# Relational graph convolution on one core: dense block products in float32r, 512 columns wide, on rows split into two parts

## What is computed

```python
h = x @ W                                       # GCN layer
deg_inv_sqrt = where(deg > 0, rsqrt(max(deg, 1)), 0)
out = segment_sum(h[src] * (deg_inv_sqrt[src] * deg_inv_sqrt[dst])[:, None], dst)
x = layernorm(x + out)

def rgcn_layer(X, W, root, bias, gamma, beta):  # 4 of these
    h = einsum('ni,rio->rno', X, W)             # 4 relations
    agg = segment_sum(h[etype, src] * inv_deg[:, None], dst)
    out = agg + X @ root + bias
    out = elu((out - mean) * rsqrt(var + eps) * gamma + beta)
    return out + X
x = layernorm(x + rgcn_layers(x))
```

## Time and profile before

| | us |
|---|---|
| median of 3 runs | 5869.68 (5861.25 to 5871.9) |
| span of the profiled execution | 5905.4 |
| sorting, count building | to about 1400 |
| GCN pass (stretch 1404 to 2282) | 878.0 |
| relational pass 1 (2296 to 3200.7) | 904.7 |
| last pass (5004 to 5884) | 880.0 |

### The profile page before, as it was taken

One profiled execution on the slowest core, in us unless ns is written; L12 is line 12 of the kernel. 1 busy time (PEld: TensorE's weight loads), 2 busy tenths in 40 slices (PEclk: granted clock), 3 DMA queues, 4 the chain that ended last, 5 costly groups with the idle time before them and its releaser, 6 DMA issues.

```text
span 5905.4 us, 80081 instructions
## 1 busy us (share of the span) xinstructions
PE 4806.4 (81%) x20415; PEld 3355.2 (57%) x20415; DVE 3711.0 (63%) x9969; ACT 1418.0 (24%) x3629; POOL 3267.9 (55%) x3256
## 2 busy tenths in 40 slices
PE   5878876777888887888887888887888888777776
PEld 4544432345666665666664666665666665556555
DVE  7998885565666664555554555555556555566665
ACT  1046653213555551111111111111111111011011
POOL 0058871003666664666664666665666664666664
PEclk8999998999999998999998999998999998888888
DMA  1000016312555555555555555555555555444444
GB/s 49 1 1 1 1 21 228 143 61 89 159 156 161 162 158 170 161 157 155 159 157 150 162 156 159 159 155 161 155 158 155 159 159 152 144 143 145 143 140 126
DMA packets 398886, 772.61 MB, mean 131 GB/s; under 512 B 77327, under 2 KB 166113, under 8 KB 398424
## 3 DMA queue, kind: packets, MB, share of 16 engines
q0 software_dynamic: 150720, 386.19, 24.2%
q1 hardware_dynamic: 246824, 380.53, 19.2%
q10 hardware_dynamic: 1008, 1.84, 0.1%
HBM read 652.04 MB, written 115.89 MB: 130 GB/s over the span
## 4 chain that ended last, share of the span: by engine, by line
PE 65%; issue 13%; DVE 12%; another core or an unknown queue 5%; ACT 2%; DVEq 2%; DMA 1%; ACTq 0%; SPq 0%
PE psum L736 24%; PE psum L758 23%; PE psum L690 5%; PE psum L807 3%; DVE arena L1429 3%; PE psum L840 2%; PE psum L793 2%; DVE arena L1571 2%; DVE arena L1303 2%; DVE arena L1290 2%; PE psum L700 1%; DVE arena L1238 1%; PE psum L622 1%; DVE emat L1409 1%
## 5 line engine op out<-in xcount | busy, mean ns | idle before, releaser
L584 POOL DMA_INDIRECT msg<-h_table,g_rel x1880 | 1795.6, 955 | 1088.5 <-issue 419.9
L1429 DVE TENSOR_TENSOR arena<-arena,psum 128x256 f32 x2940 | 1224.7, 417 | 1434.8 <-PE psum L758 970.4
L758 PE MATMUL psum<-msg,emat 128*128 128x256 f32 x4704 | 1519.7, 413 | 547.7 <-issue 323.1
L758 PEld LDWEIGHTS psum<-msg,emat 128*128 128x128 f32 x4704 | 892.9, 202 | 1021.7 <-issue 795.6
L1409 DVE TENSOR_SCALAR emat<-iota,node,weight 128x128 f32<-128x128 f32 x2352 | 862.9, 368 | 139.4 <-issue 58.8
L736 PE MATMUL psum<-arena,emat 128*128 128x256 f32 x3200 | 908.1, 405 | 6.3 <-issue 6.1
L584 POOL DMA_INDIRECT msg<-h_table,g_src x472 | 457.0, 968 | 726.3 <-PE psum L758 591.0
L736 PEld LDWEIGHTS psum<-arena,emat 128*128 128x128 f32 x3200 | 647.5, 204 | 134.0 <-issue 35.5
L566 POOL DMA_INDIRECT placed_rows<-leaving,idx x300 | 439.6, 1465 | 423.3 <-issue 416.7
L584 POOL DMA_INDIRECT hout<-h_table,g_rel x472 | 451.3, 956 | 275.4 <-issue 110.2
L793 PE MATMUL psum<-arena,emat 125*128 125x453 f16 x2000 | 448.0, 358 | 85.9 <-DVE arena L1303 85.9
(11 more groups left out here) (253 smaller groups left out, 5331.1 us busy)
## 6 DMA issues: line engine op xcount, KB each, us to landing
emat<-count_blocks SPq DMA_DIRECT2D x496, 256.0 KB
more_blocks<-count_blocks SPq DMA_DIRECT2D x372, 256.0 KB
count_blocks<-emat SPq DMA_DIRECT2D x200, 256.0 KB
h_table<-hout SPq DMA_DIRECT2D x100, 512.0 KB
msg<-h_table,g_rel POOLq DMA_INDIRECT x1880
arena<-h_table SPq DMA_DIRECT2D x24, 512.0 KB
msg<-h_table,g_src POOLq DMA_INDIRECT x472
hout<-h_table,g_rel POOLq DMA_INDIRECT x472
```

The source lines that it names most:

```text
L584: pool.indirect_dma_start(out=slots[n % RING], out_offset=None, in_=table[:, :], in_offset=bass.IndirectOffsetOnAxis(ap=rows[:, t:t + 1], ...
L758: pe.matmul(agg_ps[n % NPS][:, 0:D], emat[:, n % BODY, :], slots[n % RING], start=True, stop=True).then_inc(s_mm, 1)
L1429: dve.tensor_tensor(a, a, agg_ps[n % NPS][:, 0:D], ALU.add).then_inc(s_acc, 1)
```

## The change

- The dense products of passes 1 to 4 are in float32r, and so are `cache` and the count blocks. A row of `h` is split into a high part (its upper bits, by a mask of 12 low bits) and the rest, which lie side by side in `cache[:, chunk, relation, 2, 256]`. One product of 512 columns does both. There are 28 a window as before.
- They are issued in two halves: relations 0 and 1 (14 products, tiles d+1 to d+7), relations 2 and 3 (14 products, d+10 to d+16), in window 0 tiles 14 to 16 and 19 to 21. Each relation takes a bank of its own (512 columns), and the second half waits until DVE has read the first.
- DVE adds eight times 256 columns a window instead of four: four after tile d+8 (17 in window 0), four at the place where all four stood (`done_at[j] - 5`; in window 0 one tile before the end).
- In each of these passes, in window 0 at tiles 3 to 16, the split: for each of the 7 chunks DVE masks 1024 columns, ACT copies them into `cache`, DVE subtracts. The loads of the chunks have a semaphore each.
- The dense chunks are chosen with at most 4096 edges each (what is above may form a second chunk of the same window). So at most 26321 edges instead of 28000 are dense: NT is 600 instead of 588, DT 304 instead of 318. The choice is a loop of seven steps of small operations, and marking the edges has seven more scans over 800 columns.
- X1 is not loaded whole, but in 25 pieces of 128 KB in the last pass; the SP's loop there is unrolled. The SBUF tensors of the early stages share their place with `cache` and the count blocks; `emat` has 16 slots.
- The dense products of the GCN pass are as before.

The diff, cut to its core:

```diff
-    NDE = E * K // NW
+    MOST = 1 << 12
+    NDE = min(MOST * f + (K - f) * (E - MOST * f) // NW for f in range(K + 1))
...
+    HI_MASK = -(1 << 12)
...
+        cache = sb("cache", [P, K, R, 2, D], f32r)
...
+        counts = sb("counts", [P, K, R * P], f32r)
+        blocks = [counts[:, k, :] for k in range(K)]
+        raw_blocks = [b.bitcast(f32) for b in blocks]
...
+        masked = hout[:, 1, :].rearrange("p (r d) -> p r d", r=R)
+        x1_slots = [hout[:, 2, k * D:(k + 1) * D] for k in range(2)]
...
-        def dense_tile(j, i):
+        def dense_tile(q, j, i):
             d = done_at[j - 1] if j else 0
-            return d + 1 + i * 16 // (K * R) if j else 14 + i * 7 // (K * R)
+            if q == 0:
+                return d + 1 + i * 16 // (K * R) if j else 14 + i * 7 // (K * R)
+            h, k = divmod(i, K * R // 2)
+            if j == 0:
+                return (14, 19)[h] + k * 3 // (K * R // 2)
+            return d + (1, 10)[h] + k * 7 // (K * R // 2)
+
+        def pair_at(j):
+            return done_at[j - 1] + 8 if j else 17
+
+        def dense_at(q, j):
+            return done_at[j] - (1 if q and j == 0 else DA)
...
-                        sp.dma_start(hcaches[i], h_views[q % 2][bass.ds(c, 1), :, :, :]
-                                     .rearrange("w p r o -> (w p) r o")).then_inc(s_hc, 16)
+                        sp.dma_start(cache[:, i, :, 1, :].bitcast(f32),
+                                     h_views[q % 2][bass.ds(c, 1), :, :, :]
+                                     .rearrange("w p r o -> (w p) r o")).then_inc(s_hc[i], 16)
...
-                if q == 1:
-
+                if q == L:
                     sp.wait_ge(s_x1w, (NW + ONE0) * 16)
-                    sp.dma_start(X1.rearrange("p (w d) -> p w d", w=NW),
-                                 x1_dram.rearrange("(w p) d -> p w d", p=P)).then_inc(s_x1, 16)
...
+                def fetch_x1(j):
+                    v = window_at(mybir.EngineType.SP, j)
+                    if j >= 2:
+                        sp.wait_ge(s_fin, (j - 2) * NFIN + 2)
+                    sp.dma_start(x1_slots[j % 2], x1_view[bass.ds(v, 1), :, :]
+                                 .rearrange("w p d -> (w p) d")).then_inc(s_x1[j % 2], 16)
...
             def dense_product(q, j, i):
-                n, (c, r) = q * NW + j, divmod(i, R)
+                n = q * NW + j
+                if q:
+                    half, k = divmod(i, K * R // 2)
+                    c, r = divmod(k, 2)
+                    if i == 0:
+                        pe.wait_ge(s_dense, n)
+                    elif k == 0:
+                        pe.wait_ge(s_dstep, (n - NW) * (2 * R - 1) + R)
+                    if half == 0 and r == 0:
+                        pe.wait_ge(s_counts[c], (n + 1) * 16)
+                        if j == 0:
+                            pe.wait_ge(s_split, (q - 1) * K + c + 1)
+                    of = 2 * half + r
+                    mm = pe.matmul(dense_ps[r], blocks[c][:, of * P:(of + 1) * P],
+                                   cache[:, c, of, :, :].rearrange("p s d -> p (s d)"),
+                                   start=(c == 0), stop=(c == K - 1))
+                    if half == 0 and k == K * R // 2 - 1:
+                        mm.then_inc(s_pair, 1)
+                    if half == 1 and r == 1:
+                        mm.then_inc(s_used, 1)
+                    return
+                c, r = divmod(i, R)
...
-                if q:
-                    to, first = dense_ps[r // 2][:, r % 2 * D:(r % 2 + 1) * D], r % 2 == 0
-                    last = r % 2 == 1
-                    rows = hcaches[c][:, r, :]
-                else:
-                    to, first, rows = dense_ps[0][:, 0:D], r == 0, hcache0[c]
-                    last = r == R - 1
-                mm = pe.matmul(to, blocks[c][:, r * P:(r + 1) * P], rows,
-                               start=(c == 0 and first), stop=(c == K - 1 and last))
+                mm = pe.matmul(dense_ps[0][:, 0:D], raw_blocks[c][:, r * P:(r + 1) * P],
+                               hcache0[c], start=(c == 0 and r == 0),
+                               stop=(c == K - 1 and r == R - 1))
...
+            def high_parts(q):
+                for c in range(K):
+                    act.wait_ge(s_masked, (q - 1) * K + c + 1)
+                    act.copy(cache[:, c, :, 0, :], masked).then_inc(s_high, 1)
...
+            for i in range(K):
+                done(dve.scalar_tensor_tensor(place[:, :], taken[:, :], float(-MOST),
+                                              misc_ps[:, 256:256 + NW], ALU.mult, ALU.add))
+                done(dve.tensor_scalar(place[:, :], place[:, :], 0.0, float(MOST),
+                                       ALU.max, ALU.min))
+                done(dve.scalar_tensor_tensor(size_key[:, :], place[:, :], 32.0, iota[:, 0:NW],
+                                              ALU.mult, ALU.add))
+                done(dve.tensor_reduce(best[:, :], size_key[:, :], AXX, ALU.max))
+                dve.scalar_tensor_tensor(chosen[:, :], size_key[:, :], best[:, :], iota[:, 0:NW],
+                                         ALU.is_equal, ALU.mult, accum_out=top[:, K - 1 - i:K - i])
+                done(dve.scalar_tensor_tensor(order[:, :], size_key[:, :], best[:, :],
+                                              taken[:, :], ALU.is_equal, ALU.mult,
+                                              accum_out=part_of[:, K - 1 - i:K - i]))
+                done(dve.scalar_tensor_tensor(taken[:, :], size_key[:, :], best[:, :],
+                                              taken[:, :], ALU.is_equal, ALU.add))
...
                 done(dve.tensor_scalar(hits[2], s_hi, top[0:EP, i:i + 1], float(i + 1),
                                        ALU.is_equal, ALU.mult))
-                done(dve.tensor_tensor(d_place, d_place, hits[2], ALU.add))
+                done(dve.tensor_scalar(hits[1], hits[2], 1.0, None, ALU.min))
+                done(dve.tensor_tensor_scan(runs[2], one_row, hits[1], row_first[0:EP, i:i + 1],
+                                            ALU.mult, ALU.add))
+                done(dve.scalar_tensor_tensor(hits[2], runs[2], top_rank[0:EP, i:i + 1], hits[2],
+                                              ALU.is_le, ALU.mult))
+                done(dve.tensor_tensor(d_place, d_place, hits[2], ALU.max))
...
-            def dense_added(q, j):
+            def pair_added(q, j, half):
                 n, v = q * NW + j, window_at(mybir.EngineType.DVE, j)
                 a = cols(acc, v * D, D)
-                dve.wait_ge(s_used, (n + 1) * K)
-                dve.wait_ge(s_acc, ACC0 + q * NT + done_at[j] - DA)
-                if q == 0:
-                    dve.tensor_tensor(a, a, dense_ps[0][:, 0:D], ALU.add).then_inc(s_dense, 1)
+                base = (n - NW) * (2 * R - 1)
+                if half:
+                    dve.wait_ge(s_used, (n + 1) * K)
+                    dve.wait_ge(s_acc, ACC0 + q * NT + dense_at(q, j))
                 else:
-                    for r in range(R):
-                        if r:
-                            dve.wait_ge(s_dstep, (n - NW) * (R - 1) + r)
-                        s = dve.scalar_tensor_tensor(
-                            a, dense_ps[r // 2][:, r % 2 * D:(r % 2 + 1) * D],
-                            cols(inv, v + r * NW, 1), a, ALU.mult, ALU.add)
-                        s.then_inc(s_dstep if r < R - 1 else s_dense, 1)
-                dve.wait_ge(s_dense, n + 1)
+                    dve.wait_ge(s_pair, n - NW + 1)
+                    dve.wait_ge(s_acc, ACC0 + q * NT + pair_at(j))
+                for i in range(half * R, (half + 1) * R):
+                    r, part = divmod(i, 2)
+                    if i > half * R:
+                        dve.wait_ge(s_dstep, base + i)
+                    s = dve.scalar_tensor_tensor(
+                        a, dense_ps[r % 2][:, part * D:(part + 1) * D],
+                        cols(inv, v + r * NW, 1), a, ALU.mult, ALU.add)
+                    s.then_inc(s_dstep if i < 2 * R - 1 else s_dense, 1)
+                if half:
+                    dve.wait_ge(s_dense, n + 1)
+                else:
+                    dve.wait_ge(s_dstep, base + R)
...
+            def cache_mask(q, c):
+                dve.wait_ge(s_hc[c], q * 16)
+                dve.wait_ge(s_high, (q - 1) * K + c)
+                dve.tensor_scalar(masked.bitcast(i32), cache[:, c, :, 1, :].bitcast(i32),
+                                  HI_MASK, None, ALU.bitwise_and).then_inc(s_masked, 1)
+
+            def cache_rest(q, c):
+                dve.wait_ge(s_high, (q - 1) * K + c + 1)
+                dve.tensor_tensor(cache[:, c, :, 1, :], cache[:, c, :, 1, :].bitcast(f32),
+                                  cache[:, c, :, 0, :].bitcast(f32), ALU.subtract
+                                  ).then_inc(s_split, 1)
...
                 steps = {}
+                if q:
+                    for c in range(K):
```

(8 more changed lines are left out.)

157 lines of the change are left out of this document (96 added, 61 removed).

## The result

The changed kernel takes **5999.98 us** (5998.48 to 6008.08, 4 runs) against 5867.16 before (4 runs): ratio 1.0232, 95% interval 1.0219 to 1.0244. It is 2.3% slower. 5550 was forecast, with a chance of 0.20 for slower.

A forecast was written before the change was run, and what follows sets the result against it. PE was taken to pace the windows' dense-product stretch, a mix the rest. -267 - 85 + 36 - 22 + 18 = -320 took the profiled 5905.4 us to 5585, forecast as 5550 against the median; range 5400 to 5880.

The forecast's parts named there:

- Part 1: Dense products: one float32r product of 512 columns takes 0.215 us; PE's work falls by 6.0 us a window.
- Part 2: Four more DVE adds a window, 2.6 us, at tile d+8; second half's wait 0 to 1.5 us.
- PE waiting at tile d+10 for DVE: Sign of a wrong forecast: PE held at the second half of the dense products by DVE's adds.
- Part 3: Window's stretch with dense products: 17.8 us, between PE's 15 and POOL's 20.6; window 30.6 us, -89 a pass.
- region A: Stretch of a window where the dense products lie: some 21.9 us, PE busy 20.9, taken as paced by PE.
- part 6: Twelve more tiles a pass: nothing in the relational passes, +18 us in the GCN pass; X1's loads at 0.
- Parts 4 to 6: Split in the heads 0, other end 64 us; early stage +36, building of counts -22; twelve more tiles +18.
- POOL paces every window: Rival: tiles run at POOL's 1.25 us throughout, 775 us a pass, about 5410 in all; chance 0.12.
- DVE's in-order queue decides: Rival: four chained adds at tile d+8 hold DVE's queue; window 37.6 us, 6230; chance 0.13, shared with unhidden split.
- The float32r and the clock rival: Dense products need two readings, about 6045, or f32's rate, near 7060, 0.06; PE's clock drops between them, 6100, 0.03.
- P: Later theory, from the follow-up runs: POOL paces the windows, 24 gathers of 1.25 us, 30.0 us a window.

The follow-up runs named there:

- The late half: Changed kernel with the second half of the dense products at tiles d+12 to d+18 instead of d+10 to d+16: 5363.67 us, ratio 1.0229, second kind of chip.
- the products alone: Kernel before plus float32r products in two halves, eight adds and the split, old choice of chunks, 588 and 318 tiles: 5254.31 us, ratio 1.0036, second kind.
- K = 8 and the old choice: Kernel before plus float32r products, eight adds, split, eight dense chunks, old choice of chunks: 5726.91 us (0.9761) on the first kind, 5193.77 (0.992) on the second.
- relieved of gathers: Kernel before with every fourth gather of the relational passes left out: 5056.82 us, ratio 0.9655, second kind of chip.

## Why the prediction was wrong

**Part 1 (the products) was right.** 0.23 us measured for 0.215 taken, one instruction each. PE's busy time in 24 windows fell by 71 us where 144 were forecast; with the clock at 0.86 for 0.97 the same instructions last longer, and a row lasts 0.39 to 0.58 us though the next starts 0.23 later, which counts as busy wherever a pause follows. A float32r product of 256 columns takes 0.12 us, a float32 one 0.43. The Trainium skill's "FP8 and Floating Point Precision", TensorE Precision Notes, says that true FP32 takes four passes through the array, and of reduced-precision FP32 only that it is truncated; the ratio of 0.43 to 0.12, 3.6, fits four passes against about one.

**Part 2 (the adds) named the place and underpriced it.** The second half's wait for the adds was put at 0 to 1.5 us a window. It is 94.7/24 = 3.9 on the first kind, 43.8/24 = 1.8 on the second. The working let DVE start its adds as soon as the first half was done, with two tiles of PE's work to cover them. With four banks DVE may be four tiles behind, and on the first kind the late completions keep it there. "PE waiting at tile d+10 for DVE" stood among the prediction's own signs of being wrong.

**Part 3 failed, and it carries the error.** It let PE's saving shorten region A to 17.8, the middle between PE's 15 and POOL's 20.6, and so the window from 34.3 to 30.6; that middle had no row behind it. The window went to 838.5/24 = 34.9. The text itself had the warning: the last pass, with less PE work, is no shorter. A stretch in which PE is busy 95% is bound by PE only if PE's saving can't be refilled by a wait for another. On the second kind the failure is plain: POOL's 1.25 us a tile paces both kernels, what PE saves is hidden, and what matters is the number of tiles. There part 6 would have been the sum's largest term: "POOL's floor has them already" put twelve tiles at nothing in the relational passes, and they cost 15 us in each. On the first kind, where the forecast was measured, the same step failed, but what took its place is only read from the trace: 52 us less waiting of DVE for PE, 120 us more of PE for DVE, in 24 windows, and twelve tiles more.

**Parts 4 to 6 outside of the windows.** The split cost little: 18 us for the products and the split together on the second kind, at most 5 a pass (end taken 0, other end 16). The early stage up to L1232 is 38 us longer, 36 forecast:

```profile
64.54 0.37 DVE L1226 TENSOR_SCALAR arena<-arena 125x800 f16<-125x800 f16 x1
64.95 1.88 DVE L1227 TENSOR_TENSOR_SCAN arena<-arena,row_first 125x800 f32<-125x800 f32 x1
66.87 1.05 DVE L1229 SCALAR_TENSOR_TENSOR arena<-arena,top_rank 125x800 f16<-125x800 f32 x1
```

The building of counts gave back 14, not 22: 304 tiles from 923.7 to 1413.5, 1.61 each. The GCN pass cost 23.8 for 18. These two together are +46.4 of the loss, where the forecast had +32.

**The rivals.** "POOL paces every window" was right for the second kind, as a mechanism; as a number (5410) it was wrong, since it gave POOL's pace to the changed kernel and not to the one before. "DVE's in-order queue decides", at 0.13, named the sign, the place and the engine, with 6230 where it takes the full price and 5900 to 5970 where PE's gain pays; the result, 6000, lies between. No run on the first kind shows that DVE's queue is the cause, and on the second, where the ratio is the same, it wasn't: what this rival got right may be luck. The float32r and the clock rival: the product has its one reading; the clock fell to 0.86 behind the new waits, which on the second kind (0.95) cost nothing.

**What stays open.** On the first kind of chip no theory is shown. The late half and the products alone never ran there; that PE's wait and the lower clock make the loss there is read from the trace only. Against it stands that a window grew by the same 0.5 us on both kinds (34.3 to 34.8, and 29.4 to 29.9, measured between normalisations), which half a tile more a window at 1.25 us would explain alone. But P doesn't hold there in the form it has on the second kind either: only 78% of the gathers follow within 1.35 us, before and after, and 24 of them are 30 us of a window of 34.8. Nor is it known why the first kind is 12% slower than the second with the same program. And the form with two products of 256 columns, which needs no second adds and no wait, wasn't tried with K = 8 and the old choice, where by these runs it should do best.

## What to carry to other kernels

Before pricing a saving on the busiest engine, work out for every engine the time of one unit of the loop (here 24 x 1.25 us of gathers against 34.3) and ask what a window would be with that engine at zero; leaving out a quarter of another engine's work is a cheap run that tells. If an operation is made cheaper by giving it more output, price the reading of that output on the engine that drains it, and the wait that a smaller share of banks brings. Spend a hidden gain where the bound is: here the cheaper products paid only when they replaced gathers. That an eighth chunk needs them was not run. An estimate says so: relieved of gathers, PE with float32 products fills a window of 27.7 us; four more products at 0.43 make 29.4, as long as a window of the kernel before on that kind.

## What the runs showed of the hardware

- One program, 12% apart by chip: the kernel before takes 5866 us on one kind and 5236 to 5244 on the other. The engines' instructions have the same durations (0.95 + 0.30 for a gather, 0.42 for a tile add). What differs is when others see PE's completions. On the first kind the add at 3434.52 above began 5.6 us behind the end of its product's row, and in the relational passes 503 of 2352 tile adds before and 322 of 2400 after began 0.7 us or more behind both their product's row and DVE's work ahead of them ("remote" waits of 57.7 us in 24 windows are such, and part of the 135.0). On the second kind none did, in either kernel. The cause wasn't found.
- A float32r product of 512 columns takes 0.23 us and one of 256 columns 0.12, beside weight loads of 0.19 us that stay hidden.
- Of the split's two operations on DVE, the mask (L1687) goes with slower gathers and the subtraction (L1692) doesn't. In the heads of the changed kernel on the second kind, 41 gathers with a mask beside them for 0.15 us or more took 0.95 to 1.49 us, 1.31 in the middle, and 16 with the subtraction alone took 0.94 to 0.95. Two of the first and, last, one of the second, with DVE's operations:

```profile
2226.80 1.32 POOL L630 DMA_INDIRECT msg<-h_table,g_rel  x1 [0.30 <-issue]
2229.66 1.48 POOL L630 DMA_INDIRECT msg<-h_table,g_rel  x1 [0.30 <-issue]
2232.78 0.95 POOL L630 DMA_INDIRECT msg<-h_table,g_rel  x1 [0.30 <-issue]
...
2227.31 0.68 DVE L1687 TENSOR_SCALAR hout<-cache 128x1024 int32<-128x1024 int32 x1
2230.83 0.83 DVE L1687 TENSOR_SCALAR hout<-cache 128x1024 int32<-128x1024 int32 x1
2232.77 1.26 DVE L1692 TENSOR_TENSOR cache<-cache 128x1024 fp32r<-128x1024 f32 x1 [0.53 <-ACT cache L1020]
```
